# Loading each stage's first data in the stage before it, and a layer normalisation moved into channel attention's last pass

## The reference

```
1  x1 = x + alpha * softmax((x Wq^T)(c Wk^T)^T / sqrt(512)) (c Wv^T) Wo^T        # context attention
2  h  = Wqkv_i z + Winj_i u  for the two halves i of the features                # z = x1, u = context, as [256, 512]
   prob = softmax((q + bias) k^T / 8), 16 heads of 64, over 512 feature columns  # channel attention
   x  = Wo (prob v) + bo + z
   x2 = (x - mean(x, axis=tokens)) * rsqrt(var(x, axis=tokens) + 1e-5)           # for every feature, over 256 tokens
3  x3 = x2 + selfattention(layernorm(x2)); x4 = x3 + crossattention(layernorm(x3), context)   # 16 heads of 32
4  x5 = x4 + gelu_tanh(layernorm(x4) W1 + b1) W2 + b2                            # 512 -> 2048 -> 512
5  out = recurrent block (token shift, a recurrence over 256 steps per head, gated output, then its channel mix)
```

## Time and profile before

| | us |
|---|---|
| median of three runs | 3933.54 (3931.42 to 3935.23) |
| the profiled execution's own time | 3925.65 |
| its span in the trace | 3923.7 |

### The profile page before, as it was taken

How to read it: one execution, slowest core, us unless ns; L and a number is a source line. 1 busy time by engine, 2 the same in 40 slices (tenths; PEclk the granted TensorE clock), 3 DMA queues, 4 the chain that set the end, 5 groups by cost and what they waited for, 6 DMA issues and landing times. The chain is left out here.

```text
span 3923.7 us, 61889 instructions
## 1 busy us (share of the span) xinstructions
PE 3475.4 (89%) x23616; PEld 2678.3 (68%) x23616; DVE 2354.8 (60%) x2915; ACT 1816.2 (46%) x4207; POOL 1995.9 (51%) x1018
## 2 busy tenths in 40 slices
PE   8979999999999999589989994999867888888876
...
DMA packets 108138, 189.84 MB, mean 48 GB/s; under 512 B 13409, under 2 KB 32097, under 8 KB 106721
## 3 DMA queue, kind: packets, MB, share of 16 engines
...
...
## 5 line engine op out<-in xcount | busy, mean ns | idle before, releaser
L825 POOL TENSOR_TENSOR l_pr<-l_pr,l_inv 128x1024 f32<-128x1024 f32 x256 | 479.5, 1894 | 370.6 <-DVE l_inv L885 370.6
L734 ACT ACTIVATE l_pr<-l_ps_s,l_top 128x512 f32<-128x512 f32 x512 | 347.2, 691 | 335.2 <-DVE l_top L881 280.0
L1255 POOL TENSOR_TENSOR tok_pr<-tok_pr,tok_ma 128x1024 f32<-128x1024 f32 x128 | 305.3, 2408 | 281.5 <-DVE tok_pr L1620 281.5
L2374 POOL TENSOR_TENSOR rec_rs<-rec_sE,rec_rT 128x1024 f32<-128x1024 f32 x128 | 321.9, 2516 | 241.8 <-DVE rec_sE L2761 235.9
L820 POOL TENSOR_TENSOR l_x_lo<-l_zu,l_x_hi 128x2048 fp32r<-128x2048 f32 x63 | 288.5, 4580 | 238.6 <-ACT l_x_hi L718 238.6
L881 DVE TENSOR_REDUCE l_top<-l_ps_s 128x2 f32<-128x1024 f32 x256 | 301.3, 1219 | 11.9 <-PE l_ps_s L582 11.9
L2761 DVE TENSOR_TENSOR_SCAN rec_sE<-rec_wE,rec_ps_v 128x1024 f32<-128x1024 f32 x128 | 292.7, 2287 | 4.9
L592 PE MATMUL l_ps_t<-l_ident,l_pr 128*128 128x128 f32 x2048 | 275.4, 278 | 5.8 <-POOL l_pr L825 3.1
L592 PEld LDWEIGHTS l_ps_t<-l_ident,l_pr 128*128 128x128 f32 x2048 | 223.6, 141 | 79.2 <-issue 63.5
L1501 ACT ACTIVATE tok_pr<-tok_pr,tok_shift 128x256 f32<-128x256 f32 x512 | 253.5, 498 | 12.6 <-DVE tok_shift L1628 11.8
L739 ACT ACTIVATE l_pT<-l_ps_t 128x512 f32<-128x512 f32 x256 | 153.5, 600 | 82.6 <-PE l_ps_t L592 82.6
...
## 6 DMA issues: line engine op xcount, KB each, us to landing
l_zu<-x SPq DMA_DIRECT2D x64, 512.0 KB, 3.7
l_zu<-in_c SPq DMA_DIRECT2D x64, 512.0 KB, 4.6
l_w_raw<-in_L_w_qk SPq DMA_DIRECT2D x16, 512.0 KB, 6.8
tok_xs<-x SPq DMA_DIRECT2D x16, 512.0 KB, 3.9
x<-tok_xb SPq DMA_DIRECT2D x16, 512.0 KB, 2.8
l_xt<-in_xT SPq DMA_DIRECT2D x8, 512.0 KB, 6.2
l_ct<-in_cT SPq DMA_DIRECT2D x8, 512.0 KB, 7.2
l_xn<-in_x SPq DMA_DIRECT2D x8, 512.0 KB, 4.8
```

The lines of the kernel that those rows point to most:

```text
L734: act.activation(pr[t][:, h, :], ps_s[:, t % 2, h, :], ACT.Exp, bias=top[:, t, h:h + 1], accum_out=mass[:, t, h:h + 1]).then_inc(exped, 1)
L825: pool.tensor_tensor(pr[t][:, :, :], pr[t][:, :, :], inv[:, t, :].unsqueeze(2).to_broadcast([P, 2, FEAT]), ALU.mult).then_inc(scaled, 1)
L1255: pool.tensor_tensor(tile, tile, ma[u][:, :, :].rearrange("p t k -> p (t k)").unsqueeze(1).to_broadcast([P, 2, TT * TOK]), ALU.add).then_i ...
L2374: pool.tensor_tensor(rs[j % 2][:, :, :], sE[j % 2][:, :, :], rT[s][:, :, :], ALU.mult).then_inc(rs_made, 1)
```

## The change

- `Ahead` holds three SBUF tensors that outlive the blocks: rows of 512 KB and two pieces of 1 MB. `AheadSignals` are the semaphores of the loads into them, which `clear(keep)` leaves alone. SP issues the next block's first loads before a block ends: for channel attention x1 and the context of batch 0 and both halves of w_qk (after batch 0's store and the last loads of context attention), for the token attentions the weights of Q and K, and x2 of batch 0 once its store has landed, for the MLP x4 of batch 0 and the first two column pieces of w1, for the recurrent block x5 of batch 0. The next block uses these tensors in place of its own.
- Channel attention normalises batch n (0 to 6) within unit 9 + n of the last pass. DVE adds the two token tiles (`sum_tokens`, one 128x512 addition, right behind the unit's `add`), so that PE's mean is one matmul; means and variances stand ahead of the unit's mixing on PE; DVE subtracts the mean, ACT squares both tiles in one instruction, POOL adds the two squares, DVE copies the variance. Five logarithms are taken in one instruction at unit 15. The wait on `centred` and `var_kept` is put ahead of the next unit's transposes, since the means and variances use their banks. Behind the last pass only batch 7 goes through these steps; then POOL multiplies batches 0, 1, 5 and DVE 2, 3, 4, 6, 7.
- The token attentions, the MLP and the recurrent block are written out: no hardware loop is left in them.
- The MLP splits the two column pieces in its prologue; the other twelve halves of 512 KB (in the order in which batch 0 needs them) are rounded and split two a step in steps 0 to 5 of batch 0. The loads of the halves go through three buffers of 512 KB. The rings of the gelu lie in the two pieces. Columns are issued first, then three halves, then the biases; ACT waits for all three behind the two pieces' rounding, POOL only behind its first power.
- In the recurrent block the columns are a load and a semaphore of their own, issued first, for which ACT and DVE wait. The other seven loads are waited for by PE at "XX0" and by ACT at "K0", where the products of head sums and u (L2529) now stand.

The diff, cut to its core:

```diff
-    def clear(self):
-
-        self.nc.clear_and_free_semaphores(self.taken)
-        self.taken = []
+    def clear(self, keep=()):
+        self.nc.clear_and_free_semaphores([s for s in self.taken if s not in keep])
+        self.taken = list(keep)
         self.nc.all_engine_barrier()
...
+    def __init__(self, nc, rows_ctx, ctx):
+        self.rows = rows_ctx.enter_context(nc.sbuf_tensor("ahead_rows", [P, TT, FEAT], F32))
+        self.pieces = [ctx.enter_context(nc.sbuf_tensor(f"ahead_piece{i}", [P, FT, FEAT], F32)) for i in range(2)]
+
...
+
+    def __init__(self, semaphores, block):
+        self.piece_loaded = [semaphores.allocate(f"{block}_piece_loaded{i}") for i in range(2)]
+        self.rows_loaded = semaphores.allocate(f"{block}_rows_loaded")
+        self.all = self.piece_loaded + [self.rows_loaded]
...
+            sp.wait_ge(stored[0], 16 * PAIRS)
+            for src, a in enumerate((x1, c)):
+                sp.dma_start(ahead.pieces[1][:, 2 * src:2 * src + 2, :], a[0, :, :].rearrange("(t p) n -> p t n", p=P)).then_inc(following.rows_loaded, 16)
+            for part in range(2):
+                sp.dma_start(ahead.pieces[0][:, 2 * part:2 * part + 2, :].rearrange("p s n -> p (s n)"), w_after[0, :, part, :]).then_inc(
+                    following.piece_loaded[part], 16)
             for u in range(2):
                 store(PAIRS, u)
...
+        def normalises(g, b):
+
+            return g == COUPLES and b > BATCH
...
+            def store(b, by, count, signal):
+                sp.wait_ge(normed[by], count)
+                sp.dma_start(batch_rows(out, b), acc[:, b, :, :]).then_inc(signal, 16)
+
+            store(0, 0, 1, first_stored)
+            store(2, 1, 1, stored)
+            store(3, 1, 2, stored)
+            store(1, 0, 2, stored)
+            store(4, 1, 3, stored)
+            sp.wait_ge(first_stored, 16)
+            sp.dma_start(ahead.rows[:, :, :], batch_rows(out, 0)).then_inc(following.rows_loaded, 16)
+            store(5, 0, 3, stored)
+            store(6, 1, 4, stored)
+            store(7, 1, 5, stored)
+            sp.wait_ge(stored, 16 * (BATCH - 1))
 
         @block.tensor
...
                     pe.wait_ge(turned_kept[h], of(g, b, QT, t - 1))
+                    if t == 0 and normalises(g, b - 1):
+                        pe.wait_ge(*((var_kept, b - BATCH - 2) if h == 0 else (centred, b - BATCH - 1)))
                     for m in range(QT):
...
+            def means(n):
+
+                pe.wait_ge(mean_made, 1)
+                pe.wait_ge(presummed, n + 1)
+                if n < BATCH - 1:
+                    pe.wait_ge(turned_kept[1], of(COUPLES, BATCH + 1 + n, QT, QT - 1))
+                pe.wait_ge(centred, n)
+                pe.matmul(ps_t[1][:, :, :].rearrange("p a b -> p (a b)"), mean_of[:, :], token_sum[:, :],
+                          start=True, stop=True).then_inc(means_summed, 1)
+
+            def variances(n):
+
+                if n < 0:
+                    return
+                pe.wait_ge(sq_summed, n + 1)
+                if n == BATCH - 1:
+                    pe.wait_ge(exped, of(COUPLES, UNITS - 1, 2 * QT, 2 * QT - 1))
+                    bank = ps_s[:, 0, 0, :]
+                else:
+                    pe.wait_ge(turned_kept[0], of(COUPLES, min(BATCH + 2 + n, UNITS - 1), QT, QT - 1))
+                    pe.wait_ge(var_kept, n)
+                    bank = ps_t[0][:, :, :].rearrange("p a b -> p (a b)")
+                pe.matmul(bank, mean_of[:, :], square[:, 0, :], start=True, stop=True).then_inc(vars_summed, 1)
...
                     keys(g, b + 2)
+                if normalises(g, b):
+                    variances(b - BATCH - 2)
...
+            def squares(n):
+                act.wait_ge(centred, n + 1)
+                act.wait_ge(vars_summed, n)
+                act.activation(square[:, :, :], acc[:, n, :, :], ACT.Square).then_inc(squared, 1)
+
+            def logarithms(first, end):
+                act.wait_ge(eps_made, 1)
+                act.activation(var[:, first:end, :], var[:, first:end, :], ACT.Ln, bias=eps[:, 0:1]).then_inc(logged, 1)
+
+            def roots(first, end, logs):
+                act.wait_ge(logged, logs)
+                act.activation(var[:, first:end, :], var[:, first:end, :], ACT.Exp, scale=-0.5).then_inc(rooted, 1)
 
             round_inputs(1, 0)
...
+                if g == COUPLES and b == UNITS - 1:
+                    act.wait_ge(var_kept, EARLY)
+                    logarithms(0, EARLY)
...
+                if normalises(g, b):
+                    squares(b - BATCH - 1)
...
+            def sum_squares(n):
+                pool.wait_ge(squared, n + 1)
+                pool.tensor_tensor(square[:, 0, :], square[:, 0, :], square[:, 1, :], ALU.add).then_inc(sq_summed, 1)
+
+            def normalise(n, roots):
+                pool.wait_ge(rooted, roots)
+                pool.tensor_tensor(acc[:, n, :, :], acc[:, n, :, :], var[:, n, :].unsqueeze(1).to_broadcast([P, CT, FEAT]),
+                                   ALU.mult).then_inc(normed[0], 1)
 
             pool.wait_ge(x_split, of(1, 0, 1, 0))
...
+            def sum_tokens(n):
+                dve.wait_ge(added, of(COUPLES, BATCH + n, CT, 1))
+                dve.wait_ge(means_summed, n)
+                dve.tensor_tensor(token_sum[:, :], acc[:, n, 0, :], acc[:, n, 1, :], ALU.add).then_inc(presummed, 1)
+
+            def centre(n):
+                dve.wait_ge(means_summed, n + 1)
+                for m in range(CT):
+                    ins = dve.tensor_tensor(acc[:, n, m, :], acc[:, n, m, :], ps_t[1][:, :, :].rearrange("p a b -> p (a b)"), ALU.subtract)
+                ins.then_inc(centred, 1)
+
+            def keep_variances(n):
+                if n >= 0:
+                    dve.wait_ge(vars_summed, n + 1)
+                    dve.tensor_copy(var[:, n, :], ps_t[0][:, :, :].rearrange("p a b -> p (a b)")).then_inc(var_kept, 1)
+
...
                     split_w(1, weights_at(g, b) + 2)
+                if normalises(g, b):
+                    keep_variances(b - BATCH - 2)
...
+                if g == COUPLES and b >= BATCH:
+                    sum_tokens(b - BATCH)
...
+            centre(BATCH - 1)
+            for n in (2, 3, 4):
+                normalise(n, 1)
+            for n in (6, 7):
+                normalise(n, 2)
...
-                with eng.Fori(g0 + 1, g0 + HALFWAY - 1) as g:
+                for g in range(g0 + 1, g0 + HALFWAY - 1):
...
+            def load_ahead():
+
+                sp.wait_ge(stored, at(PASSES, 2, -1, 16))
+                sp.wait_ge(biased, at(PASSES, 2, 0))
+                sp.wait_ge(normalised, at(PASSES, 2, 0))
+                sp.dma_start(ahead.rows[:, :, :], tiles(layers[-1].out, 1, 0)).then_inc(following.rows_loaded, 16)
+                for i in range(2):
+                    sp.wait_ge(w_split["VO"[i]], len(layers))
+                    sp.dma_start(ahead.pieces[i][:, :, :], weight_columns(w1_after, i)).then_inc(following.piece_loaded[i], 16)
 
             def finish():
...
+    HALVES = [(n, i, k) for n, i in (("w2", 0), ("w1", 2), ("w2", 1), ("w1", 3), ("w2", 2), ("w2", 3)) for k in range(2)]
...
-            with eng.Fori(1, PASSES) as g:
...
+            def load_half(k):
+                n, i, half = HALVES[k]
+                if k >= 3:
+                    sp.wait_ge(half_split, k - 2)
+                if n == "w1":
+                    source = w1_d[2 * half * P:2 * (half + 1) * P, i * FEAT:(i + 1) * FEAT]
+                else:
+                    source = w2_d[(4 * i + 2 * half) * P:(4 * i + 2 * half + 2) * P, :]
+                sp.dma_start(stages[k % 3], source.rearrange("(t p) n -> p t n", p=P)).then_inc(half_loaded[k % 3], 16)
...
+            for k in range(3):
+                load_half(k)
             sp.dma_start(b1_sb[:, :], b1).then_inc(cols_loaded, 16)
             sp.dma_start(b2_row[:, :], b2.to_broadcast([P, FEAT])).then_inc(cols_loaded, 16)
-            for i in range(PIECES):
-                if i >= 3:
-                    sp.wait_ge(piece_split, i - 2)
...
+            for k in range(3, len(HALVES)):
+                load_half(k)
+                if k == 4:
+                    load(1)
...
+            power(0)
+            pool.wait_ge(cols_loaded, 48)
...
+                    if b == 0 and n == 7:
+                        pool.wait_ge(half_split, len(HALVES))
+                        add_bias(b)
...
+            def hidden(b, n):
+                if b == 0 and n in (0, 2):
+                    pe.wait_ge(piece_split, n // 2 + 1)
+                elif b == 0 and n in (4, 6):
+                    pe.wait_ge(half_split, halves_up_to("w1", n // 2))
...
+                if b == 0 and k % 2 == 0:
+                    pe.wait_ge(half_split, halves_up_to("w2", k // 2))
...
-                for i in range(PIECES):
-                    act.wait_ge(piece_loaded[i % 3], 16 * (i // 3 + 1))
```

(41 more changed lines are left out.)

485 lines of the change are left out of this document (227 added, 258 removed).

## The result

The changed kernel takes 3883.98 us (median of four runs, 3882.37 to 3885.55) against 3932.48 us of the kernel before in the same series (3927.5 to 3935.23): a ratio of 0.9878, 95% interval 0.9861 to 0.9895, 48.5 us less. The forecast was 3871 with a range of 3854 to 3892.

A forecast was written before the change was run, and what follows sets the result against it. TensorE, busy 3475.4 of 3923.7 us, was taken as the bound, with holes at stage starts as target. Terms 6.4 + 18.4 + 6 + 19 + 12 = 61.8 gave 3871.7 against the median, stated as 3871, range 3854 to 3892.

The forecast's parts named there:

- the prediction's own case: Whole kernel: the summed terms hold, forecast 3871, range 3860 to 3886 from bounds added half way; chance 0.56.
- three signs of being wrong: Units 9 to 15 over 21 us each, MLP steps 0 to 5 over 6, or "issue" gaps in written-out stages.
- Context to channel attention: Start of channel attention: with its four loads landed beforehand, inputs and weights are ready earlier; gain 6.4 us, bounds 5 and 7.
- the chain named: Channel attention's start: ACT rounds inputs and weights from 210.2, DVE takes both remainders; ready at 216.9.
- The tail: Normalisation behind channel attention's last pass: 42.3 us replaced by 14.1 (13 to 17), so 28 removed.
- The sentence on the table load: Normalisation's tail: trace shows 1.28 us a load, the skill about 2.7; by that price the new tail is 1.4 longer.
- The last pass: Channel attention, units 9 to 15: normalisation work moved there adds 10 us, bounds 4 and 17.
- Rival A: Last pass pays more, as transposes wait for subtraction and variance copy: 25 in place of 10, 3887 us; chance 0.14.
- Start of the token attentions: Next stage's start keeps its length but for 0.4 us, since small columns, issued 0.43 earlier, are still waited for.
- Loops: Writing out removes two token-attention back-edge stalls of 2.8: gain 6 us, bounds 4 and 8; nothing in MLP or recurrent block.
- MLP's start: Token to MLP: early loads and batch 0's new order bring its last addition earlier; gain 19 us, range 12 to 22.
- Recurrent block: Its start: DVE no longer awaits all eight loads, first weight product comes earlier; gain 12 us, bounds 10.5 and 13.

The follow-up runs named there:

- the first trace: Profiled execution of the changed kernel in its first series, against the kernel before: median 3883.98 us, ratio 0.9878.
- the second: Trace of the same changed kernel, run again unaltered in the last series beside the kernel before: 3881.47 us, ratio 0.9875.

## Why the prediction was right or wrong

The direction and the range held: 3883.98 in 3854 to 3892, 13 us above the forecast. Two terms were too favourable. That the time lies even within 3860 to 3886, the range of the prediction's own case, is luck: against the profiled executions, on which its terms were worked out, the sum was 18.8 us too large, and against the medians it is 13 only because the execution profiled before lay 7.9 us below the median used. The prediction named three signs of being wrong, and two of them came: units 9 to 15 over 21 us each (22.2), and steps 0 to 5 of the MLP's batch 0 over 6 (ACT's first keeps of the steps lie 6.7 apart on average, 17.61 to 57.59 behind the stage's first instruction for six steps, the 6.27 wait included). The third, "issue" gaps in the written-out stages in place of the back edges' 2.8, did not. By its own steps:

- **Context to channel attention**, 6.4 forecast: 5.0 in the first trace, 6.9 in the second, 8.0 given back without the early loads. Right, and by the chain named: all remainders 7.1 behind the start, forecast 6.9; the first product 6.0 us nearer to it (12.2 to 6.2).
- **The tail**, 28 forecast: 26.7. Right in size. It is 16.2 long where 14.1 was forecast, and the terms listed for the 14.1 add up to 12.9 to 13.3 only. Measured against them: mean 1.10 (0.47), variance 2.07 (0.47, two rows and at the lower clock), POOL's addition 1.55 (0.95 to 1.3), exponentials 1.48 (1.6), multiplications 4.50 (4.4), and some 0.4 of hand-overs. So the two matmuls, priced at half their rows, are most of the miss. The 2.2 for a multiplication was a mean of two lengths: of the four that make up L999's 8.79 in the earlier trace rows, the two beside POOL's take 3.25 and 3.36, the two behind them 1.21 each; in the new tail's last pair it is 3.36 and 1.23. The sentence on the table load took the Trainium skill's 2.7 us for the load: that section (ScalarE: Activation LUTs, "What ACT_TABLE_LOAD costs") counts 1.28 for it and 1.38 for a drain. The trace agrees with the first and shows nothing of the second: the load at 1621.47 begins 0.02 behind the activation before it, and the next begins at 1622.76, 0.01 behind its end.
- **The last pass**, 10 forecast: 19.3. This is the step that failed, a term mis-sized in both its parts, with the mechanism right. "Mean 0.47 (a quarter of L682's 1.88 for four)": the four rows listed in the earlier trace rows are two matmul calls of two rows each, so one matmul is 0.9. With that the two cost 1.8 a unit, not 0.94. "`sum_tokens` (0.74)" took 1.64 ahead of the maxima, and gave a stall of 1.56 a unit. The seven intervals grew by 2.6, five times 3.4 (3.5 for one) and -0.5, the measured 19.3. Rival A had nearly this size (25, with the chain in a row) but another cause; the waits that it names cost nothing once the sum is moved.
- **Start of the token attentions**, 0.4: 1.5 in one trace, -0.4 in the other. Within the spread.
- **Loops**, 6: layer 1 gave 5.3, of it 45.6 - 42.3 = 3.3 at the edge's batch (most of the rest lies between batches 5 and 6, 57.5 to 55.6; written out alone it is 56.0, and no run shows its cause), layer 2 1.6 at the higher clock (its edge's batch 46.5 - 43.7 = 2.8, and two others that had been 0.9 shorter are not any more) and -2.1 at the lower; 6.5 by medians in the kernel before written out. Right in size. Nothing in MLP and recurrent block: right, and the rule of the Trainium skill's "Runtime: NRT & Kernel Launch", section "Instruction fetch mechanics", that a taken branch out of the window stalls, agrees with the token edges alone; at the other four edges writing out saved nothing (341.8 to 342.1 and 781.0 to 781.2). Whether their targets lie in that window, no run shows.
- **MLP's start**, 19 forecast: 11.8. The second failing step. Up to the first output the forecast holds (29.7 behind the start forecast, 30.1 measured). It failed in carrying this gain of 21 to the last addition less 2 alone, with "each of steps 0 to 5 carries two halves ... so steps run at 5.1 to 5.5" as the only burden: from the first output on batch 0 takes 9.0 longer than before. Left out was that batch 1's normalisation stands in the same DVE queue behind these splits, and that TensorE takes up its transposes ahead of the outputs. That is the 6.27 wait, of which 3.7 could be had back by moving the transposes. And 3.7 of the 9.0 are busy time of TensorE at the lower clock (0.89 in place of 1.00). The biases are no part of the miss: ACT had them 8.7 behind the start, where 11.1 was assumed (2420); issuing them first gains a further 2.3 up to batch 0's end.
- **Recurrent block**, 12 forecast: 13.1. Right, with the wait for the seven loads as the next limit (first product forecast 12.7 behind the start, measured 12.5).

Against the profiled execution the sum was 61.8 and 43.0 came. The 18.8 missing are 9.3 in the last pass, 7.2 at the MLP's start, 2.8 in the loops with the clock at their end, 1.4 at channel attention's start, 1.3 in the tail and 0.7 in small stretches, less 1.6 by which context attention happened to end sooner, 1.1 in the recurrent block and 1.1 in the token attentions' start.
